# A megakernel's planner: the ready step with the longest chain of work left goes first, not the one that is fewest steps along

## The chip, the cores and the metric

One core of a Trainium2 chip. The metric is the device time in microseconds (us) of one execution of the whole program; the median of several runs is given. TensorE is PE, VectorE is DVE, ScalarE is ACT, GpSimd is POOL, and SyncE (SP) issues nearly all DMAs.

## What is computed

Four layers of gated cross-attention and gated feed-forward over 8 batch rows of 256 tokens by 128 features, in float32:

```python
x = x + jnp.tanh(g_xattn[l]) * xattn_l(_layernorm(x), ctx_1024, ...)
x = x + jnp.tanh(g_ffn[l]) * ffn_l(_layernorm(x), ...)
```

- Attention 0: 16 heads of 8, with an additive matrix of 256 x 256 and a mask. Attention 1: 16 heads, keys and queries normalised and turned (RoPE), causal. Attention 2: 4 query heads of 32 over one key head, with a mask per key. Attention 3: 16 heads, no mask.
- Feed-forward 0: each token takes the one of 8 matrices that a router picks. Feed-forward 1: a shared 128-512-128 MLP plus two low-rank experts per token. Feed-forward 2: one of 8 matrices 128 x 512 with an exact gelu, then 512 x 128 and a normalisation. Feed-forward 3: an MLP of 1024, its result scaled and added to the first 512 tokens (rows 0 and 1) alone.

A batch row never needs another batch row.

## The kernel before

The 8 rows are independent chains. `row_steps` (line 91) writes one row's work as a list of named steps, 173 to 180 per row: `load` (its context), `mask`, `fetch` (its x), `kv`, `k_mid`, `k_low`, `k_flip` (keys, split in three bfloat16 parts and transposed), `stats`, `norm`, `plus`, `flip`, `query`, `q_mid`, `q_low`, `q_flip` (the same of the queries), eight `max` (scores of two heads on PE, their maximum on DVE), `shift`, `shift_flip` (the maxima transposed on PE and sent by SP into the rows of the queries), eight `attend` (scores again, exponential), four `weigh` (times v), `divide`, `o_flip`, `mix` (output projection and residual), then `route`, `choose`, `spread`, `inner`, `outer` (the feed-forward; `outer` ends it), and `deep` for rows 0 and 1. Two more steps occur once: `consts` (SP loads 8 small pieces, four packs of weights and two late ones) and `fold` (DVE and ACT multiply gates and norms into weights). Attention 0 has a second DVE instruction of 128 x 1024 in every `attend`, the bias.

Each step has phases on several engines with a cost in microseconds (`COST`, line 133). There are 4 sets of row buffers (`ROWS`), so row 4 follows row 0 in the same line of work, 5 follows 1, 6 follows 2 and 7 follows 3, and within a line each engine keeps the order of the list. PSUM has 7 shared banks, taken one or two at a time; there are 4 probability buffers, 2 wide ones, 3 stacks.

`Plan.place` (line 343) plays the program before it is built: each engine has a clock; of the four lines it looks at the next step of each, and among those that are ready by then it takes one. That makes a fixed order for each engine, `plan.orders`, and the engines' programs are written in that order; every engine then runs in order and waits on semaphores. The rule for which ready step is taken is `turn_of` (line 372). Before, it is the number of the step within its row less a head start of the row, smallest first:

```python
return (step.get(s, 0) - HEAD_START[s[2]], s[2])
```

With head starts of 740, 850, 700 and 699 for rows 0 to 3 and 5, 40, 14 and 0 for rows 4 to 7, and fewer than 200 steps in a row, rows 0 to 3 always go ahead of rows 4 to 7, row 1 leads, row 0 follows, and rows 2 and 3 go nearly together.

The lines that the prediction names: L696 SP loads a row's context, L702 and L704 the constants, L706 the late weights; L982 PE transposes the context, L665 the key and query stacks, L969 all other matmuls; L1266 to L1268 statistics on DVE, L1378 norm, L1408 and L1412 the middle and low part, L1423 the maximum, L1305 to L1319 the fold, L1532 the layer-2 expert sum taken from PSUM (`outer`), L1453 the reciprocal of `o_flip`, L1461 the residual of `mix`. In the changed kernel these lines stand 17 further down.

Of the kernel before, what the change touches and what calls it, by code (L numbers as in the profile page):

```python
# [22 lines left out]
BATCH = 8  # L23
# [67 lines left out]
def row_steps(row):  # L91

    def keys(l):
        if l > 3:
            return [[]] * 5
        wide = l != 2
        return [[("kv", l, row)], [("k_turn", l, row)] if l == 1 else [], [("k_mid", l, row)] if wide else [],
                [("k_low", l, row)] if wide else [], [("k_flip", l, row, g) for g in range(2 if wide else 1)]]

    k = keys(0)  # L100
    begin = [("load", 0, row)]
    out = [("mask", 0, row), ("fetch", 0, row)] + k[0] + k[2] + k[3] + k[4] + [("bias", 0, row)]
    for l in range(4):
        wide = l != 2
        pairs, sums = (8, SETS) if wide else (2, 1)
        out += [("stats", l, row), ("norm", l, row), ("plus", l, row), ("flip", l, row), ("query", l, row)]
        out += [("q_turn", l, row)] if l == 1 else []
        out += [("q_mid", l, row), ("q_low", l, row)] if wide else []
        out += [("q_flip", l, row, g) for g in range(2 if wide else 1)]
        out += [("next", 0, row)] if l == 3 else []  # L110
        out += [("max", l, row, p) for p in range(pairs)]
        out += [("shift", l, row), ("shift_flip", l, row)]
        for p in range(pairs + AHEAD):
            out += [("attend", l, row, p)] if p < pairs else []
            out += [("weigh", l, row, (p - AHEAD) // 2)] if p >= AHEAD and (p - AHEAD) % 2 else []
        out += [("divide", l, row), ("o_flip", l, row), ("mix", l, row)]
        if l < 3:
            k = keys(l + 1)
            out += k[0] + [("stats", 4 + l, row)] + k[1] + [("norm", 4 + l, row), ("plus", 4 + l, row), ("flip", 4 + l, row)] + k[2]
            out += [("route", l, row)] + ([("gate", l, row)] if l == 1 else []) + k[3] + [("choose", l, row)] + k[4]  # L120
            out += [("spread", l, row)]
            out += [[], [("inner", l, row), ("again", l, row)], [("inner", l, row), ("lift", l, row)]][l]
            out += [("outer", l, row)] + ([("finish", l, row)] if l == 2 else [])
    if row < TAIL_ROWS:
        out += [("stats", 7, row), ("norm", 7, row), ("plus", 7, row), ("flip", 7, row)] + [("deep", 3, row, i) for i in range(2)] + [("deep_out", 3, row)]
    return begin, out + [("store", 0, row)]


AHEAD = 2
HEAD_START = [740, 850, 700, 699, 5, 40, 14, 0]  # L130


COST = {"load": [("SP", .4), ("PE", .4), ("ACT", .27), ("DVE", 1.55), ("POOL", .7)], "mask": [("SP", .4)], "fetch": [("SP", .8)], "consts": [("SP", 3)],
# [29 lines left out]
LANDS = {"consts": CONSTS, "load": 4, "mask": 4, "fetch": 4, "shift_flip": 3.4, "store": 2}  # L163
HOP = {"PE": .32, "DVE": .14, "ACT": .16, "POOL": .12, "SP": .1}
# [3 lines left out]
def phases(s):  # L168

    own = COST.get(s[:2], COST[s[0]])  # L170
    if s[0] == "attend" and s[1] != 2 and s[3] == 0:
        own = [(e, us + PLACING) if e == "ACT" else (e, us) for e, us in own]
    return own
# [71 lines left out]
def takes(s, eng):  # L245

    kind, l, row = s[:3]
    out = []
    if eng == "PE":
        out += [(use, ring, until) for use, ring, until in psum_uses(s)]  # L250
    if kind == "attend" and eng == ("DVE" if l == 0 else "ACT"):
        out.append(("probs_in", "probs", ("weighed", l, row, s[3] // 2)))
    if kind == "attend" and eng == "PE" and s[3] == 0:
        out.append(("turn", "turn", ("sums", l, row)))
    if (kind, eng) == ("mask", "SP"):
        out.append(("mask", "wide", ("biasT_ps", 0, row)))
    if (kind, l, eng) in (("spread", 0, "DVE"), ("spread", 2, "DVE"), ("inner", 1, "ACT")):
        out.append(("wide", "wide", ("f_ps", l, row)))
    if (kind, eng) == ("deep", "ACT") and s[3] == 0:
        out.append(("wide", "wide", ("f_ps", 3, row)))  # L260
    if eng == "ACT" and ((kind in ("kv", "query") and l in (0, 3)) or kind in ("k_turn", "q_turn")):
        out.append((f"{kind[0]}s", "stack", (f"{kind[0]}T_ps", l, row, 1)))
    return out
# [63 lines left out]
class Plan:  # L327


    def __init__(self, rings):  # L330
# [9 lines left out]
                    self.value[(stage, *s[1:])] = count[stage]  # L340
        self.names = sorted(count)

    def place(self):

        lines = [[] for _ in range(ROWS)]
        for b in range(ROWS):
            held = None
            for row in range(b, BATCH, ROWS):
                begin, rest = row_steps(row)
# [8 lines left out]
        lines = [[s for s in line if s[0] != "next"] for line in lines]  # L358
# [5 lines left out]
        slots = {ring: [0.0] * n for ring, n in self.rings.items()}  # L364
        pending, former = {}, {}
        rank = {s: b for b, line in enumerate(lines) for s in line}
        step = {}
        for row in range(BATCH):
            begin, rest = row_steps(row)
            step.update({s: n for n, s in enumerate(begin + rest)})  # L370

        def turn_of(s):

            return (step.get(s, 0) - HEAD_START[s[2]], s[2])


        def fits(ring, t=None):
# [18 lines left out]
        def earliest(s, eng):  # L396

            t = {"load": BEGINS}.get(s[0], 0) if eng == "SP" else 0
            for other in starts_after(s, eng):
                if other not in ended:  # L400
                    return None
                lands = LANDS.get(other[0][0], 0) if other[1] == "SP" else 0
                t = max(t, ended[other] + HOP[other[1]] + lands)
            rings = [ring for _, ring, _ in takes(s, eng)]
            if rings == ["two", "two"]:
                free = [i for i, x in enumerate(slots["one"]) if x is not None]
                sets = [(i, j) for i in free for j in free if i + 2 <= j and i + 1 in free and j + 1 in free]
                if not sets:
                    return None
                return max(t, min(max(slots["one"][n] for n in (i, i + 1, j, j + 1)) for i, j in sets))  # L410
            if rings == ["one", "one"]:
                two = sorted(x for x in slots["one"] if x is not None)
                return max(t, two[1]) if len(two) > 1 else None
            for ring in rings:
                w = fits(ring)
                if w is None:
                    return None
                t = max(t, w)
            return t

        while todo:
            best = None
            for eng in ENGINES:
                ready = []
                for b in range(ROWS):
                    q = queues[eng, b]
                    if at[eng, b] < len(q):
                        t = earliest(q[at[eng, b]], eng)
                        if t is not None:
                            ready.append((t, q[at[eng, b]]))  # L430
                if ready:
                    now = max(clear[eng], min(t for t, _ in ready))
                    t, s = min(((t, s) for t, s in ready if t <= now), key=lambda c: turn_of(c[1]))
                    if best is None or now < best[0]:
                        best = (now, eng, s)
            now, eng, s = best
            b = rank[s]
            at[eng, b] += 1
            todo -= 1
            self.orders[eng].append(s)  # L440
            clear[eng] = ended[s, eng] = end = now + dict(phases(s))[eng]
            for use, ring, until in takes(s, eng):
                got = fits(ring, now)
                bank = "one" if ring == "two" else ring
                self.home[(use, *s[1:])] = (ring, got[0])
                self.freed_by[(use, *s[1:])] = [former[bank, i] for i in got if (bank, i) in former]
                for i in got:
                    slots[bank][i] = None
                    former[bank, i] = until
                    pending.setdefault(until, []).append((bank, i))  # L450
            for stage in signals(s, eng):
                for bank, i in pending.pop((stage, *s[1:]), []):
                    slots[bank][i] = end + HOP[eng]
# [1188 lines left out]
```

## Time and profile before

| | us |
|---|---|
| median of 3 runs | 1163.98 |
| lowest, highest | 1162.83, 1172.91 |
| profiled execution, its own time | 1158.67 |
| its span, first to last instruction | 1156.9 |
| busy in it: PE, DVE, ACT, POOL | 938.3, 794.3, 501.8, 302.9 |

The sums of the prediction are made against the profiled execution. Slices are fortieths of the span, 28.9 us each; a digit is the busy share in tenths. A "releaser" is what ended the idle time of an engine.

### The profile page before, as it was taken

Reading aid. Unit: us, or ns where it says so; the run is one execution under the profiler, and the core shown is the slowest. Engines: PE = TensorE matmul, PEld = TensorE weight load, DVE = VectorE, ACT = ScalarE, POOL = GpSimd, SP = SyncE. Lnnn points to the kernel's source line nnn. Section 1 sums busy time; section 2 is a strip of 40 time slices with the busy share of each in tenths; the row PEclk is TensorE's granted clock in tenths of the full one; section 3 lists DMA queues with packets and bytes.
Section 4 is the critical chain, followed back from the end, with each engine's and each line's share of the span. In section 5 each row is a group of like instructions: output and inputs, shape, how many; then the busy total and the mean of one; then the engine's idle time right before and its main releaser. Section 6 shows DMA issues by size and latency. Waiting matters only on the chain.

```text
span 1156.9 us, 19280 instructions
## 1 busy us (share of the span) xinstructions
PE 938.3 (81%) x7316; PEld 592.9 (51%) x7316; DVE 794.3 (69%) x1849; ACT 501.8 (43%) x760; POOL 302.9 (26%) x324
## 2 busy tenths in 40 slices
PE   4787677698998889888975887887887898998776
PEld 3442335364564467555753452355554666666533
DVE  5889888848626844856099489999786747744473
ACT  3563354352325433364082835553454234353056
POOL 3520405343123003301031221245443314010000
PEclk7787788776779889778986998797998989699969
DMA  8000000000000000000000000000000000000000
GB/s 313 15 1 2 2 2 1 1 2 1 1 2 2 2 6 11 8 2 6 1 29 2 20 19 2 1 2 1 1 4 1 1 1 2 2 1 6 0 2 16
DMA packets 11741, 14.26 MB, mean 12 GB/s; under 512 B 1604, under 2 KB 10716, under 8 KB 11396
## 3 DMA queue, kind: packets, MB, share of 16 engines
q1 hardware_dynamic: 11552, 12.88, 3.4%
q8 instruction: 61, 1.00, 0.4%
q10 hardware_dynamic: 100, 0.14, 0.1%
q14 instruction: 28, 0.23, 0.1%
HBM read 11.55 MB, written 1.05 MB: 11 GB/s over the span
## 4 chain that ended last, share of the span: by engine, by line
PE 49%; DVE 35%; ACT 8%; issue 5%; POOL 2%; DMA 1%; SPq 0%; ACTq 0%; DVEq 0%
PE banks L969 37%; DVE nm_row L1423 10%; PE pv L969 7%; DVE probs L1442 3%; PE banks L665 2%; DVE qf_row L1453 2%; ACT probs L926 2%; DVE wide L1512 2%; DVE st_row L1266 2%; DVE xn_row L1378 2%; DVE mv_row L1268 1%; POOL kss_row L759 1%; ACT qT_row L843 1%; PE banks L1023 1%; ACT probs L921 1%
## 5 line engine op out<-in xcount | busy, mean ns | idle before, releaser
L1423 DVE TENSOR_REDUCE nm_row<-banks 128x4 f32<-128x1024 f32 (+1 forms) x192 | 209.4, 1126 | 38.5 <-PE banks L969 38.0
L759 POOL TENSOR_TENSOR rstd_row<-rstd_row,neghalf 128x2 f32<-128x2 f32 x66 | 47.2, 716 | 413.4 <-DVE rstd_row L1373 297.3
L926 ACT ACTIVATE probs<-banks 128x1024 f32<-128x1024 f32 (+1 forms) x144 | 126.4, 929 | 53.4 <-PE banks L969 52.1
L969 PE MATMUL pv<-probs,vpad 128*32 128x256 f32 (+1 forms) x1536 | 111.8, 414 | 23.6 <-ACT probs L921 11.1
L969 PE MATMUL banks<-kT_row,qT_row 48*128 48x256 bf16 (+2 forms) x896 | 103.4, 328 | 32.5 <-DVE nm_row L1423 18.6
L969 PE MATMUL banks<-wide,c 128*128 128x256 f32 x512 | 126.1, 402 | 0.0
L969 PE MATMUL banks<-qT_row,kT_row 50*128 50x256 bf16 (+2 forms) x896 | 98.8, 331 | 31.6 <-ACT probs L926 7.7
L969 PEld LDWEIGHTS banks<-wide,c 128*128 128x128 f32 x512 | 99.7, 200 | 17.8 <-issue 0.7
L969 PEld LDWEIGHTS banks<-kT_row,qT_row 48*128 48x128 bf16 (+1 forms) x896 | 42.5, 121 | 100.0 <-issue 52.9
L921 ACT ACTIVATE probs<-probs 128x1024 f32<-128x1024 f32 x64 | 67.2, 1055 | 55.5 <-DVE probs L1442 53.8
L969 PEld LDWEIGHTS banks<-qT_row,kT_row 50*128 50x128 bf16 (+1 forms) x896 | 49.1, 124 | 77.4 <-issue 21.3
L969 PEld LDWEIGHTS pv<-probs,vpad 128*32 128x32 f32 x1536 | 46.8, 119 | 66.9 <-issue 34.5
L1442 DVE TENSOR_TENSOR probs<-banks,biasT_row 128x1024 f32<-128x1024 f32 x64 | 75.9, 1217 | 5.9 <-PE banks L969 5.0
L665 PE MATMUL banks<-identb,stack 128*128 128x128 bf16 x768 | 65.1, 248 | 16.6 <-DVE stack L1412 13.6
L759 POOL TENSOR_TENSOR kss_row<-kss_row,neghalf 128x32 f32<-128x32 f32 x8 | 44.4, 5544 | 116.5 <-DVE kss_row L649 116.4
L969 PE MATMUL banks<-c,wide 128*128 128x128 f32 x512 | 73.5, 304 | 0.6 <-POOL wide L817 0.6
L665 PEld LDWEIGHTS banks<-identb,stack 128*128 128x128 bf16 x768 | 55.1, 113 | 29.9 <-DVE stack L1412 18.7
L969 PEld LDWEIGHTS banks<-c,wide 128*128 128x128 f32 x512 | 68.7, 215 | 3.0 <-ACT kT_row L843 0.8
L657 ACT ACTIVATE stack<-qf_row 128x768 bf16<-128x768 f32 x48 | 40.3, 843 | 58.8 <-DVE qf_row L1387 22.1
L1378 DVE TENSOR_SCALAR xn_row<-x_row,mv_row,rstd_row 128x128 f32<-128x128 f32 x116 | 49.7, 482 | 21.0 <-POOL rstd_row L759 12.7
L953 ACT ACTIVATE wide<-banks 128x1024 f32<-128x1024 f32 x8 | 8.2, 1025 | 126.3 <-PE banks L969 126.3
L812 POOL TENSOR_SCALAR_AFFINE_SELECT probs<-probs 128x512 f32<-128x512 f32 x64 | 41.0, 654 | 80.9 <-ACT probs L926 80.3
(221 smaller groups left out, 1646.6 us busy)
## 6 DMA issues: line engine op xcount, KB each, us to landing
c<-in_c SPq DMA_DIRECT2D x1, 2500.0 KB
wide<-in_mask SPq DMA_DIRECT2D x8, 256.0 KB, 3.2
qT_row<-mT_row SPq DMA_DIRECT2D x96, 4.0 KB
c<-in_c SPq DMA_DIRECT2D x1, 1194.5 KB
xn_row<-in_ctx SPq DMA_DIRECT2D x8, 128.0 KB, 3.5
x_row<-in_x SPq DMA_DIRECT2D x8, 128.0 KB, 2.9
late<-in_late SPq DMA_DIRECT2D x2, 512.0 KB, 14.8
out<-x_row SPq DMA_DIRECT2D x8, 128.0 KB, 1.9
```

The lines of the kernel that those rows point to most:

```text
L657: return nc.scalar.activation(stack[:, :, lo:hi, :], heads(src)[:, :, None, :].to_broadcast([P, NT * HEADS, hi - lo, HD]), ACT.Copy)
L665: ins = pe.transpose(dst[:, jj * SEQ + t * P:jj * SEQ + (t + 1) * P], src[:, hh:hh + 2, :, :].rearrange("p h g d -> p (h g d)"), identb[:, :])
L759: return pool.tensor_tensor(t, t, neghalf[:, 0:n], ALU.pow)
L812: pool.affine_select(diag, diag, [[0, 2], [0, NT], [1, P]], ALU.is_ge, 0.0, base=0, channel_multiplier=-1).then_inc(sem["masked"], 1)
L921: act.activation(dst[:, :, :], dst[:, :, :], ACT.Exp).then_inc(sem["probs"], 1)
L926: act.activation(dst[:, :, 0:w], src[:, :, 0:w], ACT.Exp, scale=1.0 if l == 2 else HD ** -0.5).then_inc(sem["probs"], 1)
L969: return pe.matmul(dst, lhsT, rhs, start=start, stop=stop, **kw)
L1266: ch.link(V.bn_stats(sums[b][:, t, :], src[:, t, :]))
L1378: ins = V.tensor_scalar(xn[b][:, t, :], x[b][:, t, :], mv[b][:, t, 0:1], rstd[b][:, t:t + 1], ALU.subtract, ALU.mult)
L1423: V.tensor_reduce(nm[b][:, t, :, 2 * jp:2 * jp + 2], ps[:, :, :, 0:kn], AX.X, ALU.max, negate=True).then_inc(sem["max"], 1)
L1442: V.tensor_tensor(held(probs, "probs_in", s)[:, :, :], bank("scores_ps", s)[:, :].rearrange("p (r n) -> p r n", r=2), bt[:, None, :].to_br ...
L1453: ch.link(V.reciprocal(over, den))
```

## The change

The step counter and its head starts are gone. `work_left` computes for every phase of every step the longest chain of work that still follows it within its row, by the costs of the table: the phase's own cost plus the longest of the chains behind it, with the hop from engine to engine and the landing of DMAs. An engine takes the ready step whose chain plus the row's lead is longest. The leads are some 280 to 325 for rows 0 to 3 and -4 to 23 for rows 4 to 7. Nothing of what a step computes or costs changes, nor the buffers.

```diff
-HEAD_START = [740, 850, 700, 699, 5, 40, 14, 0]
+LEAD = [280.3, 290.2, 324.8, 314.7, 4.7, -4.1, 22.7, 13.6]
...
+    def work_left(self, lines):
+
+        left, after = {}, {}
+        for line in lines:
+            former = {}
+            for s in line:
+                for eng, _ in phases(s):
+                    ahead = [(o, e, HOP[e] + (LANDS.get(o[0], 0) if e == "SP" else 0)) for o, e in starts_after(s, eng)]
+                    if eng in former:
+                        ahead.append((former[eng], eng, 0))
+                    for o, e, lag in ahead:
+                        if o[2] == s[2]:
+                            after.setdefault((o, e), []).append((s, eng, lag))
+                    former[eng] = s
+        for line in lines:
+            for s in reversed(line):
+                for eng, us in reversed(phases(s)):
+                    left[s, eng] = us + max([lag + left[n, e] for n, e, lag in after.get((s, eng), [])], default=0)
+        return left
...
-        step = {}
-        for row in range(BATCH):
-            begin, rest = row_steps(row)
-            step.update({s: n for n, s in enumerate(begin + rest)})
-
-        def turn_of(s):
-
-            return (step.get(s, 0) - HEAD_START[s[2]], s[2])
+        left = self.work_left(lines)
+
+        def turn_of(s, eng):
+
+            return (-left[s, eng] - LEAD[s[2]], s[2])
...
-                    t, s = min(((t, s) for t, s in ready if t <= now), key=lambda c: turn_of(c[1]))
+                    t, s = min(((t, s) for t, s in ready if t <= now), key=lambda c: turn_of(c[1], eng))
```

The order of the first mixes shows the whole: before, attention 0 ends for the rows in the order 1, 0, 2, 3 and row 1 is done with all four layers (its last mix is step 352 of the 985 of PE) before rows 2 and 3 end attention 2 (414 and 420). After, the order is 2, 3, 1, 0, and the last mixes of the four rows are the steps 441, 468, 487 and 503 of PE. Of the second four, 5, 6, 4, 7 was the order and 6, 7, 4, 5 is; their last mixes were the steps 902, 962, 977 and 984 and are 942, 962, 977 and 984.

SP at the start of the program, before (a name's number is that of the row's buffers; c1 to c4 are the packs of constants):

```order
L716 DMA mrow8_row1<-in_mrow 1x256 x2
L696 DMA xn_row0<-in_ctx 128x2x128
L710 DMA wide0<-in_mask 128x2x256
L714 DMA x_row0<-in_x 128x2x128
L716 DMA mrow8_row0<-in_mrow 1x256 x2
L696 DMA xn_row2<-in_ctx 128x2x128
L696 DMA xn_row3<-in_ctx 128x2x128
L702 DMA spreads<-in_spreads 9x128 x8
L704 DMA c1<-in_c1 128x1592
L704 DMA c2<-in_c2 128x2389
L704 DMA c3<-in_c3 128x5000
L704 DMA c4<-in_c4 128x1032
```

The same place after the change:

```order
L713 DMA xn_row3<-in_ctx 128x2x128
L719 DMA spreads<-in_spreads 9x128 x8
L721 DMA c1<-in_c1 128x1592
L721 DMA c2<-in_c2 128x2389
L721 DMA c3<-in_c3 128x5000
L721 DMA c4<-in_c4 128x1032
L723 DMA late0<-in_late 128x1024
L723 DMA late1<-in_late 128x1024
L727 DMA wide0<-in_mask 128x2x256
L731 DMA x_row3<-in_x 128x2x128
L733 DMA mrow8_row3<-in_mrow 1x256 x2
L713 DMA xn_row1<-in_ctx 128x2x128
```

The contexts of rows 1 and 0 now stand behind the constants and the late weights.

PE at the start, before (the transposes of the contexts, the keys, and the first key stack of the leading row):

```order
L982 MATMUL banks<-c0,xn_row1 128x128 x2
L969 MATMUL banks<-c0,ctxT_row1 128x128 x4
L982 MATMUL banks<-c0,xn_row0 128x128 x2
L982 MATMUL banks<-c0,xn_row2 128x128 x2
L982 MATMUL banks<-c0,xn_row3 128x128 x2
L969 MATMUL banks<-c0,ctxT_row2 128x128 x4
L969 MATMUL banks<-c0,ctxT_row3 128x128 x4
L665 MATMUL banks<-identb,stack2 128x128 x16
```

And after:

```order
L999 MATMUL banks<-c0,xn_row2 128x128 x2
L986 MATMUL banks<-c0,ctxT_row2 128x128 x4
L999 MATMUL banks<-c0,xn_row3 128x128 x2
L986 MATMUL banks<-c0,ctxT_row3 128x128 x4
L999 MATMUL banks<-c0,xn_row1 128x128 x2
L999 MATMUL banks<-c0,xn_row0 128x128 x2
L986 MATMUL banks<-c0,ctxT_row1 128x128 x4
L682 MATMUL banks<-identb,stack2 128x128 x16
```

The steps are the same; rows 1 and 0, whose contexts now come last, still stand in front of the leading row's key stack.

DVE at the end of the program, before (row 4 uses the buffers row0, row 6 row2, row 7 row3):

```order
L1423 TENSOR_REDUCE nm_row3<-banks 128x2x2 x6
L1430 CAST mp_row3<-nm_row3 128x2x8 x2
L1432 TENSOR_TENSOR mp_row3<-nm_row3,mp_row3 128x2x8 x2
L1453 RECIPROCAL qf_row2<-banks 128x256
L1454 TENSOR_TENSOR xT_row2<-banks,qf_row2 128x256
L1461 SCALAR_TENSOR_TENSOR x_row2<-banks,tg,xb_row2 128x256
L1453 RECIPROCAL qf_row0<-banks 128x256
L1454 TENSOR_TENSOR xT_row0<-banks,qf_row0 128x256
L1461 SCALAR_TENSOR_TENSOR x_row0<-banks,tg,xb_row0 128x256
L1453 RECIPROCAL qf_row3<-banks 128x256
```

And after (row 5 uses row1):

```order
L1470 RECIPROCAL qf_row2<-banks 128x256
L1471 TENSOR_TENSOR xT_row2<-banks,qf_row2 128x256
L1440 TENSOR_REDUCE nm_row1<-banks 128x2x2 x3
L1478 SCALAR_TENSOR_TENSOR x_row2<-banks,tg,xb_row2 128x256
L1440 TENSOR_REDUCE nm_row1<-banks 128x2x2 x5
L1447 CAST mp_row1<-nm_row1 128x2x8 x2
L1449 TENSOR_TENSOR mp_row1<-nm_row1,mp_row1 128x2x8 x2
L1470 RECIPROCAL qf_row3<-banks 128x256
L1471 TENSOR_TENSOR xT_row3<-banks,qf_row3 128x256
L1478 SCALAR_TENSOR_TENSOR x_row3<-banks,tg,xb_row3 128x256
```

Before, three rows (6, 4, 7) are left for the last attention behind the last L1532; after, all four are, and the last row's maxima stand among the endings of the others. From the last L1532 (after the change L1549) to the end there are 19 maxima before and 24 after.

## Rows read from the trace of the kernel before

**Rows 1.** The page: busy us, two engines in 40 slices, the chain's shares by engine
```profile
PE 938.3 (81%) x7316; PEld 592.9 (51%) x7316; DVE 794.3 (69%) x1849; ACT 501.8 (43%) x760; POOL 302.9 (26%) x324
...
PE   4787677698998889888975887887887898998776
...
DVE  5889888848626844856099489999786747744473
...
PE 49%; DVE 35%; ACT 8%; issue 5%; POOL 2%; DMA 1%; SPq 0%; ACTq 0%; DVEq 0%
```
**Rows 2.** Windows: stretch, length, busy PE, PEld, DVE, ACT, POOL, clock, DMA, GB/s
```profile
74.00:205.00 131.00, 97.37 (x846) 51.53 (x846) 116.16 (x229) 54.26 (x75) 41.19 (x20) 0.83 0.01 2
205.00:580.00 375.00, 319.14 (x2216) 212.16 (x2215) 213.43 (x560) 139.16 (x228) 88.70 (x114) 0.82 0.01 3
...
680.00:840.00 160.00, 130.15 (x1090) 71.12 (x1089) 143.01 (x302) 76.32 (x113) 58.58 (x34) 0.84 0.01 2
840.00:1093.00 253.00, 225.72 (x1637) 156.56 (x1634) 150.90 (x396) 95.00 (x158) 56.06 (x89) 0.89 0.01 2
1093.00:1157.00 64.00, 41.32 (x446) 20.70 (x445) 37.96 (x63) 35.06 (x46) 2.19 (x3) 0.81 0.03 8
```
**Rows 3.** Waits: who waited for whom, us in total, times, longest
```profile
DVE qf_row L1532 <- PE banks L969: 59.2, 6, 22.8
...
PE banks L969 <- DVE nm_row L1423: 31.5, 53, 2.3
```
**Rows 4.** Timeline of SP's queue, opening: start, us, issue
```profile
4.18 0.47 SPq L710 DMA_DIRECT2D wide<-in_mask  x1
...
6.82 2.88 SPq L702 DMA_DIRECT2D spreads<-in_spreads  x8
9.74 2.00 SPq L704 DMA_DIRECT2D c<-in_c  x4
```
**Rows 5.** Windows of 2 us in the opening
```profile
12.00:14.00 2.00, 0.76 (x4) 0.35 (x2) 1.97 (x4) 0.71 (x2) 0.00 (x0) 1.00 1.07 427
...
18.00:20.00 2.00, 1.85 (x9) 1.89 (x10) 1.79 (x7) 1.11 (x2) 1.85 (x3) 0.50 1.05 450
...
28.00:30.00 2.00, 1.02 (x8) 0.73 (x8) 1.78 (x4) 1.87 (x3) 0.77 (x1) 0.50 0.23 71
```
**Rows 6.** Timeline of PE and DVE, opening: start, us, instruction, idle before and releaser
```profile
11.27 1.49 PE L982 MATMUL banks<-c,xn_row 128*128 128x128 f32 x6
...
18.14 3.75 PE L969 MATMUL banks<-c,ctxT_row 128*128 128x128 f32 x16 [5.39 <-DVE qf_row L1365]
...
22.46 0.62 DVE L1266 BATCH_NORM_STATS2 st_row<-x_row 128x6 f32<-128x128 f32 x2
...
22.60 1.89 PE L665 MATMUL banks<-identb,stack 128*128 128x128 bf16 x16 [0.70 <-DVE stack L1412]
...
24.95 0.59 DVE L1378 TENSOR_SCALAR xn_row<-x_row,mv_row,rstd_row 128x128 f32<-128x128 f32 x2
...
37.00 9.14 DVE L1423 TENSOR_REDUCE nm_row<-banks 128x4 f32<-128x1024 f32 x8 [1.85 <-PE banks L969]
...
46.77 0.17 DVE L1305 TENSOR_TENSOR wcq<-c 128x16 f32<-128x16 f32 x1
```
**Rows 7.** Groups: line, engine, operation, count, busy us, mean ns, idle before
```profile
L1423 DVE TENSOR_REDUCE nm_row<-banks 128x4 f32<-128x1024 f32 x160 | 188.4, 1215 | 31.2 <-PE banks L969 31.0
...
L953 ACT ACT_TABLE_LOAD x6 | 7.7, 1283 | 0.1
...
L933 ACT ACT_TABLE_LOAD x1 | 1.3, 1283 | 0.0
```
**Rows 8.** Timeline of DVE, end
```profile
1092.81 0.42 DVE L1532 TENSOR_TENSOR qf_row<-banks,qr_row 128x256 f32<-128x256 f32 x1 [0.30 <-PE banks L969]
...
1118.16 4.62 DVE L1423 TENSOR_REDUCE nm_row<-banks 128x4 f32<-128x1024 f32 x4 [6.30 <-PE banks L969]
```
**Rows 9.** Span and mean granted clock of the core
```profile
core 0: 1156.9 us, clock 0.838
```

## The prediction

> **What bounds the kernel now.** I read the page first [rows 1]: TensorE (PE) is busy 938.3 us (81%) of the span and VectorE (DVE) 794.3 us. The chain that ended last is PE for 49% and DVE for 35%. No engine is full, and neither sum alone sets the end. The forty slices show why: DVE stands at 8 and 9 in slices 2 to 8 and again in 24 to 28, with PE mostly at 6 to 8 beside it, and PE stands at 8 and 9 in slices 9 to 17 and 29 to 37, where DVE falls to 4 and below. So the bound changes hands. Cut by stage [rows 2]: from 74 to 205 us DVE is busy 116.16 of 131 us and PE 97.37; from 205 to 580 PE is busy 319.14 of 375 and DVE 213.43; from 680 to 840 DVE again has 143.01 of 160; from 840 to 1093 PE has 225.72 of 253; and in the last 64 us neither has more than 41.32. The reason is the program: first attention (layer 0) costs DVE much, since each pair of heads is read once for its maximum and once for its bias; the router and expert matmuls of layers 0 to 2 cost PE much. What a free order of eight rows can earn is overlap of DVE-heavy steps of some rows with PE-heavy steps of others.
> The waits agree [rows 3]: DVE waits 59.2 us in six pieces for the layer-2 expert sum of PE, and PE waits 31.5 us for banks that DVE's maxima hold. The span is 1156.9 us [rows 9], so PE stands idle 1156.9 - 938.3 = 218.6 us in all; that is what can be won, less what the DVE-bound opening must keep.
>
> **The change: what moves.** No step is added or taken away. The order changes on every engine. Four terms follow, made against the profiled execution, 1158.67 us, which lies 5.3 us under the median of the runs shown (1163.98).
>
> *Opening, a loss.* The old play loads the contexts of rows 1, 0, 2, 3 and then the constants. The new one loads rows 2 and 3, then the constants and the late weights, and rows 1 and 0 behind them. The constants issue after 9.74 us now, behind 2.9 us of spreads [rows 4]. In the new order the issues between 4.2 and 6.8 us fall out, so they start some 2.6 us earlier, at 7.1. They and the late weights are 1592 + 2389 + 5000 + 1032 + 2 x 1024 columns of 128 x 4 bytes, 6.2 MB (the order listing has the shapes). The windows show 427 GB/s at 12 to 14 us and the stream ending at 28 to 30 us [rows 5], so it takes some 17 us. Ending 2.6 us earlier it ends near 26.4, and row 1's context lands there, not before 11 us. PE and DVE have row 1's context steps in front of row 2's next ones: on PE the transpose (now done in one piece of six matmuls at 11.27) stands before row 2's key transposes, which begin at 22.60 for the leading row of the old order; on DVE the context statistics stand before the leading row's L1412, which PE's key transposes wait for. From 26.4 PE needs about 0.7 + 0.7 us for two transposes and half of 3.75 us for row 1's keys [rows 6], so row 2's key transposes begin near 30, 7 to 8 us later than now. On DVE, row 2's norm stands behind row 1's and row 0's context statistics and row 1's keys: near 33.5 where it is at 24.95 now, 12 us before the first maximum. I expect DVE's first maximum at 45.5 us, where it is at 37.00 [rows 6]: 8.5 us late. Part of it is work done ahead: before that maximum the new order also has one more statistics step (0.62 us and two shorter pieces, 1.2), one more norm (0.6), one more query with its middle and low part (0.4 us each) and the fold that begins at 46.77 now (1.8 us), together 4.8 [rows 6]. DVE is the bound there, so the net is 8.5 - 4.8 = 3.7, taken as +4. Bounds: 0 if all of it is work ahead, +15.4 if nothing is repaid (26.4 less the 11 us by which all contexts are there now).
> By the Trainium skill (DMA: Bandwidth & Descriptors, section "Queues, rings and completion order") each DMA engine consumes the descriptors of a ring in ring order, and SP has one row of rings. By that rule the context cannot overtake the constants and the wait is whole; if transfers shared the engines instead, the context would be there within about 5 us of its issue and this term would be 0. No transfer of the trace before tests it closely.
>
> *Middle, the gain.* I cut each order at every mix (end of an attention) and every outer (end of a feed-forward), 56 places, both engines at the same step. The kernel's own table of costs only divides the trace's busy time among the steps: its PE sum of 844.6 is scaled to 938.3 and its DVE sum of 773.0 to 794.3 [rows 1]. The table's split is sound where the trace has a row for it (1.13 for a maximum; the trace has 188.4 / 160 = 1.18 for the large ones [rows 7]). Of each piece I take the larger engine and add up. For the order before that is 1025 us, for the new one 1000. By parts: up to the point where DVE has done about 183 us, 187 before and 185 after. From there to the last layer-2 outer, 789 before (PE's own 740) and 755 after (PE's own 730): the excess over PE's work falls from 49 to 25. Before, the two layer-2 sums of rows 2 and 3 come together with 42 PE for 14 DVE (up to row 2's), and row 5 then runs its DVE-heavy first attention with little PE beside it (42 DVE, 27 PE); after, the four rows follow one another at 14 to 28 us. Cut only at mixes the total falls by 11 (994 to 983), only at outers by 14 (993 to 979). The coarser cuts let the engines run apart more, which they do through seven banks. I take -14, the value of the middle cut; bounds -24 x 1157/1025 = -27, and +10, since the same sum says nothing of bank waits (31.5 us of them [rows 3]) that four near rows may double by a third.
>
> *Tail, a gain.* In the last 64 us PE is busy 41.32 [rows 2], and DVE idles 6.30 us before 1118.16 [rows 8] with rows 4 and 7 alone left. After the last layer-2 outer (1092.81) 19 maxima follow now and 24 after, and 59 us of PE's work where 46 does now. So 13 us more of PE's work fill 23 idle ones. The piece itself grows by what DVE and ACT add on one another's heels: five maxima of 1.18 us, 6 us. Net -7; bounds -13 and +3.
>
> *ACT's tables.* The trace has 18 table loads at 1.283 us [rows 7] (six groups, the first and the last stand there): one at the start and 17 at each change between exponentials and one of the two gelus. Read along the new order there are 10 changes, so 7 loads or 9 us of ACT go. ACT is busy 43% and hides most; it counts where a load stands before a leading exponential. I take -1; bounds 0 and -9.
>
> **Sum.** 1158.7 + 4 - 14 - 7 - 1 = 1140.7 in the profiled execution. Against the median of runs, 5.3 more: 1146.0.
>
> TensorE's clock is granted at 0.838 of 2.4 GHz on average, half of it (1.2 GHz) where PE stood idle: PE was busy 0.76 of 2 us at 12 to 14 us and idle from then to 18, and at 18 to 20 the clock stood at half [rows 5, 9]. The longer idle opening extends that by the same 8 us, in which DVE is the bound; better filled middle pieces give some back. I take both as cancelling.
>
> **Rivals.**
> - *No difference.* The idle of PE is made of short waits inside the steps, which any order has: 53 waits for maxima make 31.5 us, 0.6 us each [rows 3]. Then middle and tail give 5 together and the opening takes 4: 1163. For it: the coarse cuts move by only 1%. Against it: 59.2 us of DVE's wait come in six pieces of 10 us, which are of order and not of latency.
> - *Slower: the opening wait is paid whole.* Place: the context step of row 1 in front of row 2's keys on PE and DVE, behind 6.2 MB. Price +15.4, if what DVE does ahead is not the work that it lacks afterwards, and if four rows in one layer then make DVE the bound without PE work beside it, so that the middle gives nothing: 1164 + 15.4 = 1179. It decides from the point where the first maximum comes later than about 50 us, or the middle gains under 5. For it: DVE has 116.16 of 131 us after the opening, so lost DVE time there is not recovered. Against: 4.8 us of its work is ahead.
> - *A larger gain.* If the excess of the fine cut is real waiting and stretches as the rest does, middle -27 and tail -13 with opening +4: 1164 - 36 - 1 = 1127. For it: the real span is 1157/1025 = 1.13 of the fine sum.
> - By the same ring-order rule of the skill but with transfers shared, the opening is free: 1142; it lies inside the forecast's own range.
>
> **Chances.** Forecast (about 1146, 1134 to 1156) 0.42; larger gain 0.15; no difference 0.22; slower 0.21. A measurement here tells about 1% from no change, that is 1152.3 to 1175.6. Faster by over 1%: the larger gain, all but a small part of the forecast and a little of the second case, 0.57. Within 1%: 0.24. Slower: 0.19. The range reaches from 1122 (both gains near their bounds) to 1178 (the slower rival), which leaves out some 2 in 10.
>
> **What would show it.** Right: SP issues the constants near 7 us; PE and DVE wait for the context of a row until 25 to 28 us; the first maximum starts at 43 to 48 us; the last layer-2 outer comes 62 to 72 us before the end, with PE busy over 50 us behind it; 11 table loads; DVE's wait for the layer-2 sum under 45 us. PE's idle falls from 218.6 to near 200. Wrong: PE's idle at 218 or above; a first maximum past 50; maxima waiting for banks over 45 us; or PE's busy time moving by over 15 us through its clock, which none of the terms holds.

## The result

The changed kernel takes 1077.58 us in the median of four runs (1068.41 to 1079.57), the kernel before 1163.4 (1161.35 to 1172.91): a ratio of 0.924, interval 0.917 to 0.930. In a second sample of six runs it was 1076.33, ratio 0.927 (0.922 to 0.931). That is 7.6% less; I had forecast 1.5% less and a range that ended at 1122. The direction was right, the size wrong by far. (One profiled execution below, that of new_lead_off10, was longer than its timed runs; nothing is read from it.)

The page after, with the lines that answer to [rows 1]:

```profile
span 1066.7 us, 19274 instructions
...
PE 880.5 (83%) x7316; PEld 573.0 (54%) x7316; DVE 787.8 (74%) x1849; ACT 493.7 (46%) x753; POOL 302.4 (28%) x324
...
PE   1778787788899998887898877787888999998686
...
DVE  3899998778666945449778999878779574554783
...
PE 43%; DVE 40%; ACT 7%; issue 6%; SPq 1%; DMA 1%; POOL 1%; DVEq 0%; ACTq 0%
```

PE is busy 57.8 us less with the same 7316 matmuls, and idle 1066.7 - 880.5 = 186.2 us where it was 218.6: 32.4 us less. So two thirds of the 90.2 us between the spans are matmuls that ran faster, one third is waiting that went. (The profiled execution of the changed kernel, 1068.41 us, is the fastest on record with the highest clock, 9.2 us under the median; that of the kernel before is 4.7 under its own. So the 90.2 stand for 85.8 between the medians.) The mean granted clock [rows 9] is now

```profile
core 0: 1066.7 us, clock 0.902
```

To see where, I cut both spans at nearly equal work of PE: where its order has 150 us of work behind it, where it has 500 (both in the units of the prediction), and at the last layer-2 outer. The windows of the kernel before:

```profile
0.00:215.00 215.00, 153.43 (x1304) 87.03 (x1306) 176.74 (x370) 99.17 (x142) 75.64 (x68) 0.82 0.13 45
215.00:649.00 434.00, 360.90 (x2578) 238.90 (x2578) 263.64 (x678) 176.96 (x278) 99.65 (x121) 0.81 0.02 5
649.00:1093.00 444.00, 382.61 (x2995) 246.25 (x2994) 315.94 (x740) 190.57 (x295) 125.38 (x132) 0.88 0.02 4
```

And after the change:

```profile
0.00:220.00 220.00, 157.42 (x1250) 93.95 (x1250) 180.88 (x394) 98.67 (x139) 75.97 (x61) 0.84 0.13 44
220.00:578.00 358.00, 315.97 (x2662) 214.41 (x2658) 249.92 (x637) 171.36 (x274) 99.04 (x131) 0.95 0.03 9
578.00:998.00 420.00, 358.55 (x2832) 240.63 (x2828) 310.46 (x749) 178.71 (x281) 125.34 (x130) 0.89 0.01 1
998.00:1067.00 69.00, 48.59 (x582) 23.99 (x581) 46.59 (x71) 44.99 (x59) 2.09 (x3) 0.92 0.04 10
```

The opening and the tail are 5 us longer each, and the middle carries everything: 76 us in the second stretch (layers 1 to 3 of the first four rows, and the start of the next rows), 24 in the third. In the second, PE's busy time fell from 361 to 316 at a clock of 0.95 instead of 0.81, and its idle time from 73 to 42. The third holds 163 matmuls fewer, 136 of which now stand in the tail, and its idle time is 61 us in both kernels: most of its 24 us is work that moved, so the second stretch is where the time was won. The waits that answer to [rows 3]:

```profile
DVE qf_row L1549 <- PE banks L986: 31.9, 6, 14.7
...
PE banks L986 <- DVE nm_row L1440: 39.2, 60, 1.8
```

DVE waits half as long for the layer-2 sum; PE's waits for banks held by maxima rose from 31.5 to 39.2, a quarter.

The opening on DVE and PE, which answers to [rows 6]:

```profile
27.79 0.62 DVE L1283 BATCH_NORM_STATS2 cst_row<-xn_row 128x6 f32<-128x128 f32 x2 [7.97 <-DMA xn_row<-in_ctx]
...
48.38 9.14 DVE L1440 TENSOR_REDUCE nm_row<-banks 128x4 f32<-128x1024 f32 x8
...
27.82 1.11 PE L999 MATMUL banks<-c,xn_row 128*128 128x128 f32 x4 [13.44 <-DMA xn_row<-in_ctx]
29.07 2.05 PE L986 MATMUL banks<-c,ctxT_row 128*128 128x128 f32 x8
...
31.36 1.63 PE L682 MATMUL banks<-identb,stack 128*128 128x128 bf16 x16 [0.25 <-DVE stack L1429]
```

And SP's queue, which answers to [rows 4]; its last line issues the contexts of rows 1 and 0:

```profile
7.65 2.00 SPq L721 DMA_DIRECT2D c<-in_c  x4
...
15.85 3.74 SPq L713 DMA_DIRECT2D xn_row<-in_ctx  x2
```

Row 1's context holds both engines until 27.8 us, and the first maximum starts at 48.38 instead of 37.00.

### The profile page after: what moved, and what is told of

It reads as the page before. It is cut to its first block, busy times and chain, and to the rows that moved or that the text cites. A ratio compares the mean times of both kernels' runs of the same rounds, so it can differ in the third digit from the quotient of the medians.

```text
span 1066.7 us, 19274 instructions
## 1 busy us (share of the span) xinstructions
PE 880.5 (83%) x7316; PEld 573.0 (54%) x7316; DVE 787.8 (74%) x1849; ACT 493.7 (46%) x753; POOL 302.4 (28%) x324
## 4 chain that ended last, share of the span: by engine, by line
PE 43%; DVE 40%; ACT 7%; issue 6%; SPq 1%; DMA 1%; POOL 1%; DVEq 0%; ACTq 0%
PE banks L986 36%; DVE nm_row L1440 13%; DVE probs L1459 5%; PE pv L986 4%; ACT probs L943 2%; DVE qf_row L1470 2%; DVE wide L1529 2%; DVE st_row L1283 2%; PE banks L682 2%; DVE xn_row L1395 1%; DVE mv_row L1285 1%; DMA xn_row<-in_ctx 1%; ACT wide L965 1%; ACT qT_row L860 1%; ACT kT_row L860 1%
## 5 line engine op out<-in xcount | busy, mean ns | idle before, releaser
L1440 DVE TENSOR_REDUCE nm_row<-banks 128x4 f32<-128x1024 f32 (+1 forms) x192 | 210.3, 1128 | 39.2 <-PE banks L986 38.6
L986 PE MATMUL banks<-qT_row,kT_row 50*128 50x256 bf16 (+2 forms) x896 | 89.9, 298 | 29.6 <-DVE nm_row L1440 15.6
L986 PE MATMUL pv<-probs,vpad 128*32 128x256 f32 (+1 forms) x1536 | 105.7, 395 | 9.8 <-ACT probs L938 6.6
L986 PE MATMUL banks<-kT_row,qT_row 48*128 48x256 bf16 (+2 forms) x896 | 92.3, 294 | 25.7 <-DVE nm_row L1440 15.7
L986 PE MATMUL banks<-c,wide 128*128 128x128 f32 x512 | 85.4, 336 | 3.7 <-POOL wide L834 3.7
L986 PEld LDWEIGHTS banks<-c,wide 128*128 128x128 f32 x512 | 79.6, 245 | 8.1 <-issue 6.4
L986 PEld LDWEIGHTS banks<-kT_row,qT_row 48*128 48x128 bf16 (+1 forms) x896 | 37.2, 108 | 84.8 <-issue 46.7
L986 PEld LDWEIGHTS banks<-qT_row,kT_row 50*128 50x128 bf16 (+1 forms) x896 | 41.0, 110 | 74.2 <-issue 25.0
L860 ACT ACTIVATE qT_row<-banks 128x1024 bf16<-128x1024 bf16 x48 | 47.9, 1022 | 29.6 <-PE banks L682 29.4
L1395 DVE TENSOR_SCALAR xn_row<-x_row,mv_row,rstd_row 128x128 f32<-128x128 f32 x116 | 44.6, 441 | 21.1 <-POOL rstd_row L809 11.5
L682 PEld LDWEIGHTS banks<-identb,stack 128*128 128x128 bf16 x768 | 50.2, 106 | 18.1 <-issue 9.9
## 6 DMA issues: line engine op xcount, KB each, us to landing
late<-in_late SPq DMA_DIRECT2D x2, 512.0 KB, 15.4
```

The source lines that it names most:

```text
L682: ins = pe.transpose(dst[:, jj * SEQ + t * P:jj * SEQ + (t + 1) * P], src[:, hh:hh + 2, :, :].rearrange("p h g d -> p (h g d)"), identb[:, :])
L860: act.activation(dst, cols, ACT.Copy, **kw).then_inc(sem[stage], 1)
L986: return pe.matmul(dst, lhsT, rhs, start=start, stop=stop, **kw)
L1395: ins = V.tensor_scalar(xn[b][:, t, :], x[b][:, t, :], mv[b][:, t, 0:1], rstd[b][:, t:t + 1], ALU.subtract, ALU.mult)
L1440: V.tensor_reduce(nm[b][:, t, :, 2 * jp:2 * jp + 2], ps[:, :, :, 0:kn], AX.X, ALU.max, negate=True).then_inc(sem["max"], 1)
```

## Experiments

**What in the change carries the gain.** It has two parts, a rule and eight numbers. The first three runs take one without the other.

```diff
-HEAD_START = [740, 850, 700, 699, 5, 40, 14, 0]
+HEAD_START = [700, 704, 718, 714, 2, -2, 9, 5]
```

> The old rule (number of the step within its row), with head starts of 700, 704, 718, 714, 2, -2, 9, 5: the new leads converted at 285 us of chain per some 175 steps. Rows go 2, 3, 1, 0 and their first mixes span 50 steps of PE, not 113. Theory A, the gain comes from how far the rows of a wave are spread and not from the rule: under 1100 us, most of the 86 us. Theory B, the gain is the rule's, since it weighs a step by the work behind it: over 1140 us, at most a quarter of the gain.

1179.57 us, ratio 1.016 (1.012 to 1.020): a little slower than before. All mixes of the first four rows stand within some ten places of the changed kernel's on PE (those of attention 0 at 95, 110, 130, 145 against 86, 110, 130, 143), and yet it takes 102 us more. Theory A falls.

```diff
-LEAD = [280.3, 290.2, 324.8, 314.7, 4.7, -4.1, 22.7, 13.6]
+LEAD = [1850.0, 2125.0, 1750.0, 1747.5, 12.5, 100.0, 35.0, 0.0]
```

> The new rule (longest chain left), with the old head starts converted to us at 2.5 us per step: 1850, 2125, 1750, 1747.5, 12.5, 100, 35, 0. Row 1 runs far ahead again, its last mix at step 352 of PE as before. Theory A (spread of the rows): over 1140 us. Theory B (the rule): under 1100 us. In between, 1100 to 1140, both have a share.

1204.51 us, ratio 1.039 (1.035 to 1.044). Theory B falls too: the new rule with the old head starts is slower than the old rule.

```diff
-LEAD = [280.3, 290.2, 324.8, 314.7, 4.7, -4.1, 22.7, 13.6]
+LEAD = [300.0, 300.0, 300.0, 300.0, 0.0, 0.0, 0.0, 0.0]
```

> The new rule with equal leads, 300 for rows 0 to 3 and 0 for rows 4 to 7, so that only the work left sets the order and rows 0 and 1 with their longer feed-forward 3 go first. Theory A (rows close together is what counts): 1075 to 1105 us. If the tuned leads themselves carry the gain (a stagger of 10 to 45 us between rows): over 1120 us.

1236.47 us, ratio 1.067 (1.064 to 1.070), the slowest of all. The page shows the same work at less than full use:

```profile
span 1234.6 us, 19271 instructions
...
PE 943.1 (76%) x7316; PEld 600.8 (49%) x7316; DVE 796.1 (64%) x1849; ACT 492.3 (40%) x753; POOL 303.2 (25%) x324
```

Neither part earned anything alone. What was left: the leads are written to a tenth, and the order they yield is one of very many. `Plan.place` ends with a time of its own, the end of the last step in its play; by it the order before has 1077.0 us, the changed one 1017.1, and these three 1100.9, 1118.8 and 1173.8. The chip ranks these five the same way. That gave theory D: the gain is the choice of one order among many by the play's own time. The next four test it; in each only the line of eight numbers differs, from the changed kernel's or, for the old rule, from the kernel before's.

```diff
-LEAD = [280.3, 290.2, 324.8, 314.7, 4.7, -4.1, 22.7, 13.6]
+LEAD = [280.05, 290.08, 324.82, 315.26, 4.74, -4.31, 22.68, 12.66]
```

> The new rule with each lead moved by up to 1 us (280.05, 290.08, 324.82, 315.26, 4.74, -4.31, 22.68, 12.66), which still sends the rows 2, 3, 1, 0 but changes some 1250 of the 2663 places in the five orders. Of twelve such draws it is the middle one in the time that the play itself gives: 1040.6 us, where the changed kernel's order has 1017.1 and the order before 1077.0. Theory D, the gain is the pick of one order among many by the play's own time, and chip time is the play's time times 1.053 to 1.077 (the six orders timed so far): 1096 to 1120 us. Theory E, rule and rough leads carry it and the last digits are idle: within 10 us of 1077.6.

1096.79 us, ratio 0.945 (0.938 to 0.952): at the lower end of D's range. Leads moved by 1 us at most cost 19 us.

```diff
-LEAD = [280.3, 290.2, 324.8, 314.7, 4.7, -4.1, 22.7, 13.6]
+LEAD = [277.79, 288.98, 324.97, 320.27, 5.12, -6.23, 22.49, 4.19]
```

> The new rule with each lead moved by up to 10 us (277.79, 288.98, 324.97, 320.27, 5.12, -6.23, 22.49, 4.19), again the middle one of twelve draws by the play's time: 1089.2 us. Theory D (the pick): 1147 to 1173 us, no better than the kernel before at 1163. Theory E (rule and rough leads): under 1110 us.

1167.67 us, ratio 1.005 (1.002 to 1.008): in D's range. Rule, rough leads and the order of the first four rows are the changed kernel's (of the last four, row 4 now ends ahead of row 7), and all of the gain is gone.

```diff
-HEAD_START = [740, 850, 700, 699, 5, 40, 14, 0]
+HEAD_START = [701.48, 705.47, 716.1, 711.45, -0.39, -7.04, 12.76, 5.03]
```

> The old rule with its head starts found by 2240 trials that keep what the play calls shorter, begun from 700, 704, 718, 714, 2, -2, 9, 5 (1100.9 us in the play, 1179.6 on the chip): 701.48, 705.47, 716.1, 711.45, -0.39, -7.04, 12.76, 5.03, at 1051.6 us in the play. Theory D (the pick): 1107 to 1133 us, so that the old rule gets a third to two thirds of the gain without the new one. Theory B' (the new rule is needed): not under 1150 us.

1129.22 us, ratio 0.972 (0.965 to 0.978): in D's range. The old rule gets 2.8% of the 7.6% by such a choice alone. Whether a longer search under the old rule would reach the changed kernel's time was not run.

```diff
-LEAD = [280.3, 290.2, 324.8, 314.7, 4.7, -4.1, 22.7, 13.6]
+LEAD = [354.04, 336.89, 283.09, 297.62, 40.59, 30.4, 22.49, 9.63]
```

> The new rule at quite other leads, found by 2160 such trials from random ones: 354.04, 336.89, 283.09, 297.62, 40.59, 30.4, 22.49, 9.63, so that rows go 0, 1, 3, 2 and the first four are further apart (71 us between first and last, not 44); 1041.9 us in the play. Theory D: 1097 to 1122 us, as new_lead_off1, though almost no step stands where it stood there. If the row order 2, 3, 1, 0 with its gaps of 10 to 24 us is what matters: over 1140 us.

1132.21 us, ratio 0.975 (0.968 to 0.981): 10 us above D's range, under the 1140 of its rival. Here the chip takes 1.087 times the play's time, the largest of all. (The expectations give 1.053 to 1.077 for the orders timed before; the kernel before itself, 1163.4 / 1077.0, is 1.080.) The old rule and the new one, each with some 2200 trials (the old begun from the converted leads, the new from random ones), came out 3 us apart (1129.2 and 1132.2), so at like effort the new rule showed no advantage. What the changed kernel has over both, 52 us and more, goes with its shorter play; how its leads were found is not on record.

All orders together, by the play's time; PE's idle and busy time and the time at half clock (twice the missing share of the mean clock, times the span) are those of the profiled execution, in us:

| order | play, us | chip, us | chip / play | PE idle | PE busy | half clock |
|---|---|---|---|---|---|---|
| changed | 1017.1 | 1077.6 | 1.059 | 186 | 881 | 208 |
| new_lead_off1 | 1040.6 | 1096.8 | 1.054 | 200 | 893 | 251 |
| new_rule_other | 1041.9 | 1132.2 | 1.087 | 209 | 920 | 308 |
| old_rule_searched | 1051.6 | 1129.2 | 1.074 | 220 | 907 | 271 |
| before | 1077.0 | 1163.4 | 1.080 | 219 | 938 | 376 |
| new_lead_off10 | 1089.2 | 1167.7 | 1.072 | not read | | |
| old_rule_new_lead | 1100.9 | 1179.6 | 1.071 | 248 | 931 | 363 |
| new_rule_old_lead | 1118.8 | 1204.5 | 1.077 | 255 | 948 | 420 |
| new_rule_equal | 1173.8 | 1236.5 | 1.053 | 292 | 943 | 431 |

The play orders them as the chip does but for one neighbouring pair, new_rule_other and old_rule_searched, which the chip has 3 us apart. Its factor to the chip runs from 1.053 to 1.087, some 3%, so it does not settle smaller differences. PE's busy time rises with the time at half clock, by (938 - 881) / (376 - 208) = 0.34 us per us between the two kernels, and by 0.28 (new_rule_equal) to 0.41 (old_rule_searched) from the changed kernel to the others. That the clock follows from PE's gaps is not shown, and the sum of PE's idle time alone does not set it: old_rule_new_lead has 29 us more of it than the kernel before, and the higher clock (0.846 against 0.838).

What a lower clock costs can be seen with the order held, since executions of one kernel differ in it. The changed kernel with the constants last was profiled twice (its two runs come further down): PE was busy 890.2 us in the one and 898.6 in the other, idle 174.2 and 173.5, and the spans were 1064.4 and 1072.1. So 8 us more of busy time made the span 8 us longer. The one:

```profile
core 0: 1064.4 us, clock 0.886
```

The other:

```profile
core 0: 1072.1 us, clock 0.882
```

Over the executions of the changed kernel itself, from 1066.7 us at 0.902 to 1078.1 at 0.878, the span grows by some 0.2 us per us at half clock. The kernel before never came above 0.849 and the changed one never under 0.878: the higher clock belongs to the order.

**The opening.** One SP step is moved and every other engine's order is kept:

```diff
         self.place()
+        sp, consts = self.orders["SP"], ("consts", 0, ROWS - 1)
+        sp.remove(consts)
+        sp.insert(sp.index(("load", 0, 0)) + 1, consts)
         count = {}
```

> The changed kernel with one DMA step moved: the constants and late weights are issued after all four contexts, the order on all other engines untouched. If the opening wait was paid as my prediction had it (first maximum 8.5 us late, half of it work done ahead): 3 to 9 us faster than the changed kernel's 1077.6, first maximum some 8 us earlier. If DVE, or something later, makes the opening's length meaningless: within 2 us of it.

1069.7 us, ratio 0.9235 (0.921 to 0.927). The first maximum came 8 us earlier:

```profile
40.28 3.68 DVE L1443 TENSOR_REDUCE nm_row<-banks 128x4 f32<-128x1024 f32 x3
```

The median was 7.9 us lower but the ratio the same as in the changed kernel's first sample, so it was run again beside it.

> The changed kernel as it is, run beside the next three so that they can be compared on one chip: 1068 to 1080 us.

> The changed kernel with the constants issued after all four contexts and nothing else moved, again, now beside the changed kernel. In its first run DVE's first maximum began at 40.28 us, where the changed kernel has 48.38, and the median was 7.9 us lower, but against another sample of the kernel before. If the opening's delay is paid whole: 6 to 10 us under changed_again. If it is covered by what comes after: within 2 us of it. My prediction had put it at 4 net.

1076.33 and 1068.26 us, ratios 0.927 (0.922 to 0.931) and 0.919 (0.915 to 0.922): 8.1 us, as much as the first maximum gained. The runs of each kernel scatter by 10 to 15 us, so this is good to some 4 us, both samples taken together: the wait does cost time, but that it is paid only by half is not ruled out by this pair. The mirror of it, in the kernel before:

```diff
+        sp.insert(sp.index(("fetch", 0, 0)) + 1, consts)
```

> The kernel before with its constants issued after the second context instead of the fourth, nothing else moved: the opening wait alone, without the new order. PE and DVE then wait for row 2's context some 15 us, and the first maximum comes 6 to 10 us later than 37.0. Paid whole: 1167 to 1171 us. Covered by later slack: within 3 us of the kernel before.

1171.68 us, ratio 1.0074 (1.004 to 1.011), 9.9 us over its own sample of the kernel before (1161.78), a little above the expected 1167 to 1171. The first maximum came 8.7 us late, and here the difference is good to some 3 us; with the 7.9 and 8.1 above, the delay is paid nearly or wholly:

```profile
45.69 9.14 DVE L1426 TENSOR_REDUCE nm_row<-banks 128x4 f32<-128x1024 f32 x8 [2.38 <-PE banks L972]
```

**A better version.** The constants' place told to the play, and the leads chosen again for it:

```diff
-            return (-left[s, eng] - LEAD[s[2]], s[2])
+            return (s[0] == "consts", -left[s, eng] - LEAD[s[2]], s[2])
...
-LEAD = [280.3, 290.2, 324.8, 314.7, 4.7, -4.1, 22.7, 13.6]
+LEAD = [280.26, 290.2, 324.73, 314.68, 4.7, -4.08, 22.71, 13.56]
```

> The new rule with one more: in the play SP takes the constants last of all that is ready, so that the whole order is planned for it, and leads picked by 4150 trials near the given ones (280.26, 290.2, 324.73, 314.68, 4.7, -4.08, 22.71, 13.56); 1017.0 us in the play, as the changed kernel's 1017.1, which counts the contexts as there either way. Theory D (the play's time times 1.05) with the real opening put right: 1062 to 1074 us, at or a little under consts_last_again. Over 1080 us, the play's last few us say nothing.

1061.87 us, ratio 0.915 (0.912 to 0.918): the fastest, at the lower edge of the expected 1062 to 1074, 14.5 us under the changed kernel beside it and 6.4 under consts_last_again. The play calls this order no better than the changed one (1017.0 to 1017.1), because its landing times do not know that a context waits behind the constants. So the play does not say where the 6.4 us come from, and whether the leads or the planned opening give them was not separated.

## Why the prediction was right and wrong

*Opening: mechanism right, price half.* I had the constants at 7.1 us (7.65 measured), row 1's context at 26.4 (27.8), the first maximum at 45.5 (48.38), and booked +4 for it. The wait alone costs about 8 us. My step from 8.5 to 4 took the 4.8 us of work done ahead as part of the delay. It is not: with the constants last that work is still ahead, and the first maximum, at 40.28, is 3.3 us later than before; the wait puts 8.1 on top of it. The bounds of 0 to 15.4 held.

The ring-order rule of the Trainium skill (DMA: Bandwidth & Descriptors, section "Queues, rings and completion order") agrees with the trace: both engines waited for the context until 27.8 us, behind 6.2 MB. Under the sharing that would have made the term 0, with my 5 us from the issue at 15.85, the context would have been there some 7 us earlier. (The last of my rivals names the ring-order rule beside that sharing; the two exclude each other.)

*Tail: right in what could be read.* The last layer-2 sum on DVE, L1549, is at 998.46 and the span ends 68 us later, inside the 62 to 72 that I named. The stretch holds 582 matmuls where it held 446, 13.6 us of PE's work more in the prediction's units, and grew by 5 us (I had 6); so it takes some 8 us from the rest, booked as -7. PE is busy 48.6 us of it and not over 50, as I had said, at a clock of 0.92 where it was 0.81.

```profile
998.46 0.42 DVE L1549 TENSOR_TENSOR qf_row<-banks,qr_row 128x256 f32<-128x256 f32 x1 [1.09 <-PE banks L986]
...
1050.58 1.76 DVE L1470 RECIPROCAL qf_row<-banks 128x256 f32<-128x256 f32 x1 [6.23 <-PE banks L986]
...
1060.66 1.76 DVE L1470 RECIPROCAL qf_row<-banks 128x256 f32<-128x256 f32 x1 [5.91 <-PE banks L986]
```

The last two rows still end alone, with the gaps that the kernel before had (6.23 and 5.91 us there too). That the tail's extra work takes 8 us from the rest follows from the sum and was not tested by itself.

*ACT's tables: count right.* Eleven loads, as read from the order; these are two of the five groups. What they are worth in time (I had -1) no run shows:

```profile
L970 ACT ACT_TABLE_LOAD x4 | 5.1, 1283 | 0.1
...
L943 ACT ACT_TABLE_LOAD x4 | 5.1, 1283 | 3.4 <-PE banks L986 3.4
```

*Middle: the step that failed.* I took "-14, the value of the middle cut", and bounded it at -27; with the tail and the tables I had -22. Middle and tail together made -95 in spans (434 + 444 + 64 us to 358 + 420 + 69). In PE's account: I had its idle time at "near 200", 18 us less, and it fell by 32.4; and I had its busy time unchanged, and it fell by 57.8. So two things were wrong, and the second is the larger.

First, the cut. At 32 mixes or 24 outers whatever order stands inside a piece counts as perfect overlap. I did the sums for all nine orders of the table. Against the medians, the sum cut at mixes has a correlation of about 0.4, at outers about 0.8, the 56-place cut that I used about 0.5, a cut at every mix, outer, key, query, route, spread and maximum (376 places) about 0.9, and the play's own time 0.97. The finest cut falls by some 50 us from the kernel before (about 1190) to the changed one, where the 56-place cut falls by 25. But no cut is safe: for old_rule_new_lead, which the chip has 1.6% slower than the kernel before, the 56-place cut says 1016 to 1025 and even the 376-place cut has it a little under the kernel before. Only the play puts it on the right side (1100.9 to 1077.0). I had argued that the coarser cuts were nearer the truth because engines run apart through seven banks. Nine orders speak against that: what separates them lies inside the pieces.

Second, the clock. "I take both as cancelling" left PE's busy time as it was. It fell by 57.8 us. My own sign of failure named it: "PE's busy time moving by over 15 us through its clock". The same 7316 matmuls ran at a mean clock of 0.902 instead of 0.838, and in the second stretch at 0.95 instead of 0.81, where 45 us of busy time went along with 31 of idle time. How the order of the waits brings the clock up stays open.

One reading of mine was wrong beside that. I wrote that PE stands at 8 and 9 in slices 9 to 17 and 29 to 37 of [rows 1] and DVE at 4 and below there. DVE stands at 8 in slices 10, 14, 17 and 30 and at 6 or 7 in seven others, and PE at 7 in slice 31. The two engines were busy together more often than I said; that the bound changes hands rests on the windows of [rows 2] alone.

The rivals: "no difference" and "slower" are out for this order. But old_rule_new_lead and new_lead_off10 (1.016 and 1.005) have the same order of the first four rows and nearly the same places of the mixes, and gain nothing, as the second rival had it: near rows by themselves earn nothing. "A larger gain" named the right direction and had 36 us for 86, without the clock. That I named no rival in which one order is picked for its total is the gap behind all this: leads with a decimal in a function that plays the whole program look like a search's result, and one step of the working should have asked what such a pick can be worth apart from the rule.

## What to carry to other kernels

When engines run fixed orders and wait on each other in pieces of about a microsecond, how far apart the rows run says little about the time: two orders whose mixes stand within some ten to twenty places of each other differed by 9%. Judge an order at the grain of its waits; if the kernel has a play of itself with costs like the trace's, its total can rank the orders to some 3%, and here picking by it moved the time where the rule alone did not. Put what the play leaves out (a load behind 6 MB of constants) into it, and where the mean clock is well under 1, as the 0.838 here, give the matmuls' speed a term and a range of its own: it made the larger part of this gain.

## What the runs showed of the hardware

The granted clock in the profile reads 1.00 from the start of the span to its first recorded change (near 36 us in the changed kernel, near 17 us in the kernel before), and this is no evidence of speed. After the change PE stood idle from 14 to 27.8 us, and the windows read 1.00 all along:

```profile
24.00:26.00 2.00, 0.00 (x0) 0.00 (x0) 0.00 (x0) 0.00 (x0) 0.00 (x0) 1.00 1.04 371
```

The eight matmuls of a context's keys at 29.07 us took 2.05 us, the same as at 9.35 us, before the idle stretch. The same eight took 1.06 us in a later window, also recorded at 1.00:

```profile
126.48 1.06 PE L986 MATMUL banks<-c,ctxT_row 128*128 128x128 f32 x8
```

The 16 key transposes at 31.36 us took 1.63 us, those at 35.92 us 1.85 us. The same 16 took 1.89 us at a recorded 0.50 in the kernel before [rows 6], and 1.07 us at a recorded 1.00 a little later in the changed kernel:

```profile
40.25 1.07 PE L682 MATMUL banks<-identb,stack 128*128 128x128 bf16 x16 [0.35 <-DVE stack L1429]
```

So PE ran near half clock there while the record said full. Up to the first recorded change the duration of a matmul tells its clock, and the column does not.
